# A decoder layer on one core: the token rows of the expert tiles, from the sixth tile on, turned by VectorE in squares of 32 instead of by TensorE

## The chip, the cores and the metric

The kernel runs on one core of one Trainium2 chip. A core has five engines that work through their own instruction streams and meet at semaphores: TensorE (PE, the matmuls), VectorE (DVE), ScalarE (ACT), GpSimd (POOL) and SyncE (SP), and 16 DMA engines that their queues feed. Data lies in SBUF (128 partitions) and the results of matmuls in PSUM (8 banks of 128 x 512 float32). The metric is the device time of the core in microseconds, smaller is better; the profile gives one execution of the program.

## The reference

A decoder layer on x of shape (8, 256, 256): self-attention with rotary embedding, cross-attention on a context of the same shape, and a feed-forward layer with 8 experts of which each token uses 2. Each of the three adds to x. The part that matters here is the third, on 2048 tokens of width 256:

```python
def _L0_ffn_ref(x, router_w, router_b, lang_w, lang_b, w1, b1, w2, b2):
    ...
    router_probs = jax.nn.softmax(router_logits, axis=-1)
    top_p, top_i = jax.lax.top_k(router_probs, TOP_K)
    top_p = top_p / top_p.sum(axis=-1, keepdims=True)
    h = jax.nn.gelu(jnp.einsum('bsd,edh->bseh', x, w1) + b1, approximate=False)
    expert_out = jnp.einsum('bseh,ehd->bsed', h, w2) + b2
    sel = jnp.take_along_axis(expert_out, top_i[..., None], axis=2)
    return (top_p[..., None] * sel).sum(axis=2)

x = x + _L0_ffn_ref(_layernorm(x, axis=-1), ...)
```

w1 is (8, 256, 1024), w2 (8, 1024, 256), all float32. The kernel computes the experts only for the tokens that chose them.

## The kernel before

Every engine walks the same table of numbered slots, made by `schedule()`, and for each slot emits its own part of the pieces that stand there. So the order of the pieces in the slots is the order of each engine's instructions; nothing is reordered later. Slots up to about 275 hold the attention of 16 units (8 batches, self and cross); the routing of the tokens and the expert tiles lie at the end.

The routing puts each token's row number on the list of its two experts. Tiles of 128 rows are cut from these lists: 39 tiles, each of one expert. Tiles 0 to 8 are cut after the first four batches, the others when all batches are routed. For tile n:

- `list` (SP): loads 128 row numbers and gates. `gather` (POOL, line 1484): an indirect DMA brings the 128 rows of width 256 into one of three buffers `x_rows`. Before it may overwrite a buffer, the turn of tile n - 3 must be over.
- `w1t` (ACT line 990 and DVE line 1270): each copies one half of the expert's w1 (128 x 1024) into one of two buffers `w1t`, reordered.
- `xturn` (PE line 857, ACT line 997): the rows have tokens on the partitions, the up-projection needs the 256 features there. TensorE turns the two halves of 128 x 128 by a product with the identity into a PSUM bank of a ring of three; ScalarE copies the bank to one of two buffers `xT`, once the up-projection of tile n - 2 is over.
- `up_a`, `up_b` (PE line 748): 32 float32 matmuls of 128 x 128, hidden = w1 x rows. They wait for `xT`, both halves of `w1t`, and the hidden bank. ACT line 1012 applies bias and gelu.
- `down_a`, `down_b` (PE line 755): 16 matmuls of 128 x 256 into a bank of the same ring.
- `moved_y` (DVE lines 1281 and 1287): adds the bias, multiplies by the gate. `add` (POOL line 1494): an indirect DMA adds the 128 rows to the output; each waits for the landing of the one before.

From slot 304 on the slots repeat, with j from 3 to 38 in slot 301 + j, in this order within a slot: list and gather of tile j + 4, w1t and xturn of tile j + 2, up of tile j + 1, down, moved_y and add of tile j. A text below says "up 5" for the up-projection of tile 5. Slot 304 also holds the last batch's `counted` (PE line 851), `table` (a chain of some 15 small VectorE instructions that ends at line 1219 and tells tiles 9 to 38 their expert and their place) and `listed` (POOL line 1424: eight indirect DMAs that write the lists), all ahead of the tile pieces.

`WARM` names places at which TensorE runs filler matmuls of the identity (line 634) whose results are overwritten; `fill()` emits them after it has the ring's bank. Among them are 4 ahead of down 6 and 10 ahead of the turn of tile 9. `Plan` numbers the uses of the ring; `filled` and `emptied` give the semaphore and the count for a use.

Of the kernel before, what the change touches and what calls it, by code (L numbers as in the profile page):

```python
# [15 lines left out]
P = 128  # L16
# [69 lines left out]
def rope_tables():  # L86
# [4 lines left out]
    for at in (position // 16, position % 16):  # L91
# [54 lines left out]
        "count", 1, 5), (8, "ot", 1, 6, 0), (2, "cturn", 1, 7), (4, "xturn", 2, 0), (5, "xturn", 2, 2), (4,  # L146
        "down_a", 2, 6), (10, "xturn", 2, 9), (8, "top", 3, 0), (3, "low", 13, 1))
AFTER_SELF = ((18, "xbias"),)
# [29 lines left out]

STEADY, STEADY_AT = 3, 304


# [98 lines left out]
class Plan:  # L280


    def __init__(self):
        self.slots = schedule()
        self.warm = {tuple(piece): many for many, *piece in WARM}
        rung = [p for s in self.slots for p in s.pieces if p[0] in RING]
        self.use = {p: i for i, p in enumerate(rung)}

        self.loaded, counts = {}, [0] * STACKS
        for unit in ORDER:  # L290
            i = POS[unit]
            counts[i % STACKS] += len(Q_LOADS) + len(K_LOADS) + (i >= MASKED)
            self.loaded[unit] = counts[i % STACKS]


class Memory:
# [128 lines left out]
    def signals(self):  # L425
# [32 lines left out]
        self.s_gather = [sem(f"tile_gather{i}") for i in range(X_RING)]  # L458
        self.s_list = [sem(f"tile_list{i}") for i in range(LIST_RING)]
        self.s_w1_v, self.s_w1_a = sem("tile_w1_vector"), sem("tile_w1_scalar")  # L460

# [154 lines left out]
def tensor_attention(m):  # L616
# [143 lines left out]
    for slot in plan.slots:  # L760
# [6 lines left out]
        for piece in slot.pieces:  # L767
# [79 lines left out]
            elif name == "counted":  # L847
# [4 lines left out]
                          stop=True).then_inc(m.fills(piece), 1)  # L852
            elif name == "xturn":
                bank = fill(piece)
# [5 lines left out]
            elif name == "up_a":  # L860
# [4 lines left out]
                if n == 1:  # L865
                    for w in range(B_RING):
                        pe.wait_ge(m.b_free[w], len(ORDER) * H // B_RING)
                pe.wait_ge(*m.emptied(("xturn", TILE, n)))
                pe.wait_ge(m.s_w1_v, n + 1)
# [29 lines left out]
def scalar_attention(m, out, rows, table):  # L899
# [45 lines left out]
    for slot in plan.slots:  # L945
        if slot.low is not None:
            exponentials(slot.low)
        for piece in slot.pieces:
# [29 lines left out]
            elif name == "w1t":  # L978
# [9 lines left out]
                else:  # L988
# [3 lines left out]
                         ).then_inc(m.s_w1_a, 1)  # L992
            elif name == "xturn":
                act.wait_ge(*m.filled(piece))
# [59 lines left out]
def vector_attention(m):  # L1054
# [176 lines left out]
    for slot in plan.slots:  # L1231
        if slot.top is not None:
            maxima(slot.top)
        for piece in slot.pieces:
# [26 lines left out]
            elif name == "w1t":  # L1261
# [6 lines left out]
                else:  # L1268
                    v.wait_ge(m.s_up, 2 * (n - 1))
                v.tensor_copy(m.w1t[n % 2][:, 1, :].rearrange("p (c q) -> p c q", c=FC),  # L1270
                              m.w1_sb[1][:, bass.ds(e, 1), :].rearrange("p a (q c) -> p (a c) q", c=FC)
                              ).then_inc(m.s_w1_v, 1)
            elif name == "moved_y":
                if n == 0:
# [77 lines left out]
def pool_attention(m, table, rows, out):  # L1352
# [112 lines left out]
    for slot in plan.slots:  # L1465
        for piece in slot.pieces:
# [8 lines left out]
            elif name == "gather":  # L1475
# [4 lines left out]
                if n == EARLY:  # L1480
                    pool.wait_ge(*m.stored(m.s_rows, B - 1))
                if n >= X_RING:
                    pool.wait_ge(*m.filled(("xturn", TILE, n - X_RING)))
# [84 lines left out]
```

## Time and profile before

| what | value |
|---|---|
| median of 3 runs | 726.67 us (723.82, 726.67, 730.84) |
| the profiled execution's own time | 728.32 us |
| its span, first to last instruction | 726.4 us |
| mean granted TensorE clock | 0.974 |
| busy: PE, ACT, DVE, POOL | 92%, 61%, 51%, 40% of the span |

Busy shares are means over the attention (to about 430 us, with some tile work from 402 us on) and the tiles (the rest). The granted clock is given as a share of 2.4 GHz; it has two levels, 1.00 and 0.50 (1.2 GHz).

### The profile page before, as it was taken

How to read it: one execution, taken by the hardware profiler on the slowest of the kernel's cores; microseconds unless marked ns; L12 is line 12 of the kernel's file. 1: busy time of each engine (PE TensorE's matmuls, PEld its weight loads, DVE VectorE, ACT ScalarE, POOL GpSimd, SP SyncE). 2: the span in 40 equal slices, each digit the busy share in tenths (PEclk: the TensorE clock that was granted, in tenths of full speed). 3: DMA queues.
4: the chain of work that ended last, by engine and by line, in shares of the span. 5: the costliest groups of instructions: out<-in, count | busy, mean ns of one | idle time of the engine just before them, and what ended most of it. 6: DMA issues, size and time to landing. Idle time of an engine off the chain costs nothing.

```text
span 726.4 us, 15766 instructions
## 1 busy us (share of the span) xinstructions
PE 670.2 (92%) x5090; PEld 526.9 (73%) x5090; DVE 367.1 (51%) x811; ACT 443.6 (61%) x880; POOL 291.4 (40%) x547
## 2 busy tenths in 40 slices
PE   7678899999999999979879799999999999999996
PEld 4445576666767666656546487888999999999995
DVE  2296787686877777758853334422222222222221
ACT  3444658576676777768536474865666666666661
POOL 4233325254332464624173363543434333333322
PEclk9799999999999999999989899999999999999999
DMA  5445355555455554774796552142212121212121
GB/s 132 145 118 161 112 132 160 143 163 154 137 138 159 167 162 149 196 206 135 221 236 79 174 148 52 23 37 41 42 33 44 31 45 31 44 30 45 30 30 23
DMA packets 55841, 78.26 MB, mean 108 GB/s; under 512 B 15374, under 2 KB 45297, under 8 KB 54737
## 3 DMA queue, kind: packets, MB, share of 16 engines
q1 hardware_dynamic: 42441, 62.37, 31.6%
q0 software_dynamic: 8512, 10.26, 9.2%
q10 hardware_dynamic: 4808, 4.61, 2.8%
q8 instruction: 43, 0.70, 0.4%
q14 instruction: 37, 0.30, 0.1%
HBM read 54.52 MB, written 22.35 MB: 106 GB/s over the span
## 4 chain that ended last, share of the span: by engine, by line
PE 70%; DVE 7%; POOL 5%; issue 5%; DMA 5%; ACT 4%; SPq 3%; ACTq 0%; DVEq 0%; POOLq 0%
PE attention_psum L748 18%; PE attention_psum L755 18%; PE attention_psum L740 7%; PE attention_psum L690 5%; PE attention_psum L709 5%; PE attention_psum L788 4%; PE attention_psum L645 3%; PE attention_psum L639 3%; DVE neg_max L1228 2%; PE attention_psum L634 2%; SPq L565 2%; DMA lists<-entry,place 2%; POOL lists L1424 1%; PE attention_psum L826 1%; PE attention_psum L857 1%
## 5 line engine op out<-in xcount | busy, mean ns | idle before, releaser
L916 ACT ACTIVATE weights<-attention_psum 128x512 f32<-128x512 f32 x256 | 147.7, 596 | 87.7 <-PE attention_psum L709 65.0
L1228 DVE TENSOR_REDUCE neg_max<-attention_psum 128x2 f32<-128x512 f32 x256 | 168.8, 685 | 54.2 <-PE attention_psum L690 53.7
L748 PE MATMUL attention_psum<-over,v 128*128 128x128 f32 x1248 | 146.4, 275 | 0.0
L748 PEld LDWEIGHTS attention_psum<-over,v 128*128 128x128 f32 x1248 | 143.1, 192 | 0.2
L755 PE MATMUL attention_psum<-weights 128*128 x624 | 143.2, 383 | 0.0
L1012 ACT ACTIVATE weights<-attention_psum,b_sb 128x128 f32<-128x128 f32 x312 | 89.0, 369 | 79.7 <-PE attention_psum L748 77.7
L1494 POOL DMA_INDIRECT out<-over x39 | 64.4, 1650 | 165.2 <-DVE over L1287 154.6
L755 PEld LDWEIGHTS attention_psum<-weights 128*128 128x128 f32 x624 | 117.0, 193 | 14.5
L690 PE MATMUL attention_psum<-weights 99*128 99x256 bf16 x512 | 99.9, 277 | 11.7 <-DVE neg_max L1228 10.9
L709 PE MATMUL attention_psum<-weights 102*128 102x256 bf16 (+1 forms) x512 | 104.0, 277 | 5.6 <-DMA weights<-maxT 4.9
L1281 DVE TENSOR_TENSOR over<-attention_psum,b_sb 128x256 f32<-128x256 f32 x39 | 16.6, 425 | 179.6 <-PE attention_psum L755 178.9
L990 ACT COPY v<-w_sb 128x1024 f32 x39 | 80.4, 2061 | 0.8 <-issue 0.6
L1503 POOL TENSOR_TENSOR weights<-weights 128x512 bf16<-128x512 f32 x32 | 36.9, 1157 | 107.4 <-ACT weights L1051 107.1
L690 PEld LDWEIGHTS attention_psum<-weights 99*128 99x128 bf16 x512 | 41.9, 99 | 51.6 <-DVE neg_max L1228 20.8
L740 PE MATMUL attention_psum<-weights,v 128*32 128x256 f32 x1024 | 76.3, 395 | 0.0
L709 PEld LDWEIGHTS attention_psum<-weights 102*128 102x128 bf16 (+1 forms) x512 | 50.3, 99 | 16.6 <-issue 5.8
L1270 DVE COPY v<-weights 128x1024 f32 x39 | 42.8, 1100 | 16.2 <-issue 14.5
L740 PEld LDWEIGHTS attention_psum<-weights,v 128*32 128x32 f32 x1024 | 31.1, 111 | 27.2 <-issue 14.9
L1484 POOL DMA_INDIRECT over<-rows,over x39 | 38.9, 998 | 23.1 <-DMA over<-lists 12.2
L634 PE MATMUL attention_psum<-identb 128*128 128x512 bf16 x168 | 43.1, 394 | 2.3 <-POOL identb L1367 2.3
L1424 POOL DMA_INDIRECT lists<-entry,place x32 | 32.9, 1027 | 15.2 <-issue 9.1
L639 PE MATMUL attention_psum<-ident,weights 128*128 128x128 f32 x160 | 25.6, 287 | 14.2 <-ACT weights L933 12.5
(168 smaller groups left out, 757.1 us busy)
## 6 DMA issues: line engine op xcount, KB each, us to landing
parts<-weights SPq DMA_DIRECT2D x96, 128.0 KB
weights<-parts SPq DMA_DIRECT2D x64, 192.0 KB
weights<-parts SPq DMA_DIRECT2D x64, 128.0 KB
weights<-in_L_ffn_w SPq DMA_DIRECT2D x8, 1024.0 KB, 9.2
weights<-parts SPq DMA_DIRECT2D x64, 64.0 KB
w_sb<-in_L_ffn_w SPq DMA_DIRECT2D x8, 512.0 KB
weights<-in_L_ffn_w SPq DMA_DIRECT2D x8, 512.0 KB
weights<-in_x SPq DMA_DIRECT2D x8, 256.0 KB, 3.2
```

The costliest lines, as they stand in the source:

```text
L634: pe.matmul(bank[:, :], m.identb[:, :], wide, start=True, stop=True)
L639: last = pe.transpose(bank[:, (c * T + t) * P:(c * T + t + 1) * P], rows[:, t, c * P:(c + 1) * P], m.ident[:, :])
L690: last = pe.matmul(bank[:, t * S:(t + 1) * S], q[0:MAX0, h % HALF, t * P:(t + 1) * P], k[0:MAX0, h % HALF, :], start=True, stop=True)
L709: last = pe.matmul(bank[:, t * S:(t + 1) * S], k[0:rows, h % HALF, t * P:(t + 1) * P], q[0:rows, h % HALF, :], start=True, stop=(i < SELEC ...
L740: last = pe.matmul(m.o_bank[32 * j:32 * j + 32, g * S:(g + 1) * S], v[:, t, head_at(h), :], m.p[:, u % P_RING, t * S:(t + 1) * S], start=( ...
L748: last = pe.matmul(m.hT_bank[j % 2][:, c * P:(c + 1) * P], m.w1t[j % 2][:, k, c * P:(c + 1) * P], m.xT[j % 2][:, k, :], start=(k == 0), st ...
L755: last = pe.matmul(m.bank_of(("down_a", TILE, j))[:, 0:D], m.hidT[j % HIDDEN][:, c, :], m.w2_sb[:, bass.ds(expert, 1), c, :].rearrange("p ...
L916: act.activation(m.p[:, u % P_RING, :], m.b_bank[u % B_RING], ACT.Exp, scale=SCALE[ORDER[u // H][0]]).then_inc(m.b_free[u % B_RING], 1)
L990: act.copy(m.w1t[n % 2][:, 0, :].rearrange("p (c q) -> p c q", c=FC), m.w1_sb[0][:, bass.ds(e, 1), :].rearrange("p a (q c) -> p (a c) q", ...
L1012: last = act.activation(m.hidT[n % HIDDEN][:, c, :], m.hT_bank[n % 2][:, c * P:(c + 1) * P], ACT.Gelu, bias=m.b1_sb[:, bass.ds(gelu_expert ...
L1228: v.tensor_reduce(m.neg_max[:, :, h:h + 1], m.a_bank[u % A_RING].rearrange("p (t k) -> p t k", t=T), AXX, ALU.max, negate=True).then_inc(m ...
L1494: pool.indirect_dma_start(out=known(out, n), out_offset=tokens(n), in_=m.y_gated[n % 2], in_offset=None, compute_op=ALU.add).then_inc(m.s_ ...
```

## The change

For tiles 5 to 38 the piece `xturn` is no longer TensorE's and ScalarE's. VectorE turns the gathered rows straight from `x_rows` to `xT` with 16 transposes: each takes the rows of 32 tokens and, in both halves of the features, 32 columns (32 partitions x 2 x 32) and writes them turned. It waits for the gather and for the up-projection of tile n - 2 once, ahead of the sixteen; the last one counts up a new semaphore. TensorE's up-projection waits for that semaphore instead of the ring's, and so does POOL's gather that reuses the buffer. These tiles' turns leave the ring of three banks, and the ten fillers ahead of tile 9's turn are deleted. Tiles 0 to 4 stay as they were.

```diff
-        "down_a", 2, 6), (10, "xturn", 2, 9), (8, "top", 3, 0), (3, "low", 13, 1))
+        "down_a", 2, 6), (8, "top", 3, 0), (3, "low", 13, 1))
...
+SQUARES = 5
+QUAD = 32
...
-        rung = [p for s in self.slots for p in s.pieces if p[0] in RING]
+        rung = [p for s in self.slots for p in s.pieces
+                if p[0] in RING and not (p[0] == "xturn" and p[2] >= SQUARES)]
...
+        self.s_squares = sem("tile_rows_turned")
... (TensorE)
-            elif name == "xturn":
+            elif name == "xturn" and n < SQUARES:
...
-                pe.wait_ge(*m.emptied(("xturn", TILE, n)))
+                if n < SQUARES:
+                    pe.wait_ge(*m.emptied(("xturn", TILE, n)))
+                else:
+                    pe.wait_ge(m.s_squares, n - SQUARES + 1)
                 pe.wait_ge(m.s_w1_v, n + 1)
... (ScalarE)
-            elif name == "xturn":
+            elif name == "xturn" and n < SQUARES:
... (VectorE)
+            elif name == "xturn" and n >= SQUARES:
+
+                v.wait_ge(m.s_gather[n % X_RING], 16 * (n // X_RING + 1))
+                v.wait_ge(m.s_up, 2 * (n - 1))
+                x = m.x_rows[n % X_RING][:, :].rearrange("p (c q) -> p c q", c=KC)
+                for r in range(0, P, QUAD):
+                    for q in range(0, P, QUAD):
+                        last = v.transpose(m.xT[n % 2][q:q + QUAD, :, r:r + QUAD], x[r:r + QUAD, :, q:q + QUAD])
+                last.then_inc(m.s_squares, 1)
... (POOL)
-                if n >= X_RING:
+                if n >= SQUARES + X_RING:
+                    pool.wait_ge(m.s_squares, n - X_RING - SQUARES + 1)
+                elif n >= X_RING:
                     pool.wait_ge(*m.filled(("xturn", TILE, n - X_RING)))
```

TensorE's order at slot 304, after down 2 and the count of the last batch. `ident` and `over` are the identity and the area that holds `x_rows` and `xT`; `v` holds `w1t`. Before:

```order
L851 MATMUL attention_psum<-before,ones 128x8 [waits counts_before,ring_free1]
L857 MATMUL attention_psum<-ident,over 128x128 [waits tile_gather2,ring_free2]
L857 MATMUL attention_psum<-ident,over 128x128
L748 MATMUL attention_psum<-over,v 128x128 [waits tile_w1_scalar,tile_gelu,tile_w1_vector,ring_free1]
L748 MATMUL attention_psum<-over,v 128x128 x15
L882 TENSOR_LOAD over [waits ring_free0]
```

And with the change, whose line numbers are 5 to 8 higher:

```order
L856 MATMUL attention_psum<-before,ones 128x8 [waits counts_before,ring_free1]
L753 MATMUL attention_psum<-over,v 128x128 [waits tile_w1_scalar,tile_gelu,tile_w1_vector,ring_free1]
L753 MATMUL attention_psum<-over,v 128x128 x15
L890 TENSOR_LOAD over [waits ring_free2]
L890 ISA x2
```

The turn of tile 5 (line 857) has gone from between the count and up 4. Up 5 and all later ones carry the wait `tile_rows_turned` in place of the ring's.

VectorE's order at the same slot, from the end of the routing table to the result of tile 3. `weights` holds w1's second half. Before:

```order
L1219 TENSOR_TENSOR over<-start,over 128x30 [waits dve_chain]
L1265 TENSOR_LOAD over [waits routed]
L1265 ISA x2
L1270 ISA [waits tile_up]
L1270 COPY v<-weights 128x1024
L1276 TENSOR_LOAD over
L1276 ISA x2
L1281 ISA [waits tile_gated,ring_full0]
L1281 TENSOR_TENSOR over<-attention_psum,b2_sb 128x256
L1287 TENSOR_SCALAR over<-over 128x256 [waits tile_add,ring_free0]
```

With the change:

```order
L1227 TENSOR_TENSOR over<-start,over 128x30 [waits dve_chain]
L1273 TENSOR_LOAD over [waits routed]
L1273 ISA x2
L1278 ISA [waits tile_up]
L1278 COPY v<-weights 128x1024
L1288 STREAM_TRANSPOSE over<-over 32x2x32 [waits tile_up,tile_gather2]
L1288 STREAM_TRANSPOSE over<-over 32x2x32 x15
L1293 TENSOR_LOAD over
L1293 ISA x2
L1298 ISA [waits tile_gated,ring_full2]
L1298 TENSOR_TENSOR over<-attention_psum,b2_sb 128x256
L1304 TENSOR_SCALAR over<-over 128x256 [waits tile_add,ring_free2]
```

The sixteen transposes stand between the weight copy of a tile and the result of the tile two before it, here and in each later slot; in slot 304 they also stand behind the whole routing table.

## Rows read from the trace of the kernel before

**Rows 1.** The page, busy time, share of the span and instructions
```profile
PE 670.2 (92%) x5090; PEld 526.9 (73%) x5090; DVE 367.1 (51%) x811; ACT 443.6 (61%) x880; POOL 291.4 (40%) x547
```

**Rows 2.** Chain that ended last, 430 to 726: start, length in us, what
```profile
446.16 5.24 PE attention_psum L755 x16
...
460.65 3.58 PE attention_psum L748 x32
...
467.91 3.57 PE attention_psum L748 x32
...
485.98 0.86 PE attention_psum L634 x4
...
490.29 2.16 PE attention_psum L634 x10
492.67 3.57 PE attention_psum L748 x32
...
499.92 3.57 PE attention_psum L748 x32
...
702.85 3.57 PE attention_psum L748 x32
...
709.88 3.57 PE attention_psum L748 x32
```

**Rows 3.** Timeline of one tile: start, us, engine, line, what, [idle before]
```profile
601.31 0.42 DVE L1281 TENSOR_TENSOR over<-attention_psum,b_sb 128x256 f32<-128x256 f32 x1 [4.94 <-PE attention_psum L755]
...
602.52 1.10 DVE L1270 COPY v<-weights 128x1024 f32 x1 [0.40 <-issue]
...
608.56 0.42 DVE L1281 TENSOR_TENSOR over<-attention_psum,b_sb 128x256 f32<-128x256 f32 x1 [4.93 <-PE attention_psum L755]
```

**Rows 4.** Timeline around slot 304
```profile
457.47 2.02 ACT L990 COPY v<-w_sb 128x1024 f32 x1
...
460.21 0.44 PE L857 MATMUL attention_psum<-ident,over 128*128 128x128 f32 x2 [1.35 <-DVE over L1281]
...
464.07 0.21 DVE L1219 TENSOR_TENSOR over<-start,over 128x30 int32<-128x30 f32 x1
465.06 1.09 DVE L1270 COPY v<-weights 128x1024 f32 x1 [0.78 <-DVE over L1219]
```

**Rows 5.** VectorE's groups by form: ... | busy us, mean ns | idle before
```profile
L1297 DVE TENSOR_TENSOR over<-weights,over 128x128 f32<-128x128 f32 x32 | 7.8, 286 | 0.0
...
L1062 DVE TENSOR_TENSOR over<-upto,over 128x64 f32<-128x64 f32 x2 | 0.5, 227 | 0.1
```

**Rows 6.** Timeline of VectorE, two operations that do not wait for one another
```profile
33.09 0.49 DVE L1297 TENSOR_TENSOR over<-weights,over 128x128 f32<-128x128 f32 x2
```

**Rows 7.** Timeline, the gather of tile 9
```profile
488.20 1.02 POOL L1484 DMA_INDIRECT over<-rows,over  x1 [0.30 <-issue]
```

**Rows 8.** Line 1484, all gathers, from issue to landing
```profile
DMA to landing us min/median/max: 2.7/2.9/5.6
```

**Rows 9.** Timeline of TensorE around idle times
```profile
362.18 0.39 PE L690 MATMUL attention_psum<-weights 99*128 99x256 bf16 x2
...
365.90 0.61 PE L690 MATMUL attention_psum<-weights 99*128 99x256 bf16 x2 [3.11 <-DVE neg_max L1228]
...
407.20 1.12 PE L857 MATMUL attention_psum<-ident,over 128*128 128x128 f32 x4 [3.56 <-DMA over<-rows,over]
408.11 0.42 PE L709 MATMUL attention_psum<-weights 99*128 99x256 bf16 x1
...
413.89 0.27 PE L709 MATMUL attention_psum<-weights 99*128 99x256 bf16 x1
...
445.13 1.03 PE L645 MATMUL attention_psum<-r_sb,rowsT 128*128 128x12 f32 x8 [1.43 <-ACT rowsT L943]
```

**Rows 10.** Windows: stretch, length, busy PE PEld DVE ACT POOL, PEclk, DMA
```profile
447.00:450.00 3.00, 3.00 (x8) 2.37 (x7) 2.07 (x12) 0.54 (x2) 0.00 (x0) 0.50 0.00 0
```

**Rows 11.** Chain that ended last, near its end
```profile
718.32 3.64 DMA out<-over
```

## The prediction

> **What bounds the kernel now.** I read the page first: TensorE is busy for 670.2 us, 92% of the span [rows 1]. That is a mean over two programs, so I went on to the chain of the work that ended last. From 460 us on it is TensorE alone: 32 matmuls of line 748 (the up-projection of a tile), 16 of line 755 (the down-projection of the tile before), again and again [rows 2]. The reader should look at the starts. Up-projection of tile 9 starts at 499.92, of tile 37 at 702.85: 28 intervals of 7.248 us. Up-projection of tile 38, ahead of which no rows are turned, starts at 709.88, so 7.03 us later. The difference, 0.218 us, is what two turns of line 857 cost on the path. The timeline of one tile then shows how much room VectorE has: it sat idle for 4.93 us before line 1281 [rows 3].
>
> **What is removed.** Tiles 5 to 38 are turned by VectorE, 34 tiles. From up 9 to up 38 there are 28 turns (tiles 11 to 38): 28 x 0.218 = 6.10 us. Between up 5 (467.91) and up 9 (499.92) lie 32.01 us, four tiles with four turns, 4 fillers of line 634 (0.86 us) and 10 more (2.16 us) [rows 2]. The ten are the ones that the change deletes. What stays is 4 x 7.03 + 0.86 = 28.98, a gain of 3.03 us. The ten were cover for the wait on the gather of tile 9. That gather is issued at 488.20 and lands 2.9 us later at the median, 5.6 at most, so by 491.1 or at worst 493.8 [rows 7, 8]. In the new order VectorE waits for it while TensorE goes on with up 8 and down 7, so no filler is needed: nothing is put back for it. ScalarE loses the copies of line 997; it waits for TensorE in any case, and I cost them at nothing.
>
> **What is added: x, the time of 16 transposes.** The trace has no VectorE transpose. Each moves 32 partitions x 64 elements. The nearest rows are the 128x64 operations at 227 ns each, one waiting for the other, and the 128x128 operations of line 1297 at 286 ns [rows 5]. Two of line 1297 that do not wait for one another take 0.49 us and not 0.57 [rows 6]: the second starts 0.20 us after the first, 0.08 less than its length. The 59 ns between 227 and 286 are the 64 extra columns, so without a wait a 64-column operation should come every 0.20 - 0.06 = 0.14 us. The sixteen write apart and wait only once. Low end: 15 x 0.14 + 0.23 = 2.3 us. If nothing overlaps: 16 x 0.227 = 3.6 us. If besides each column takes two turns: 16 x 0.286 = 4.6 us. I take x = 2.6 us, 0.16 each, near the low end, because the pair that the trace has without a wait does overlap; the rest is for filling and emptying a square. Here a page speaks against the change. The Trainium skill (VectorE: DVE Perf Modes, section "The TRN2 errata") has a fixed cost per instruction on SBUF sources that many small tiles pay each time, measured at about 150 cycles beside one cycle a column. By it x is an estimate of 16 x 214 cycles at 0.96 GHz = 3.6 us. The sum would be 10.7 - 3.6 = 7.1 us by it. The trace agrees for operations that wait for one another (227 ns) and not for the pair of line 1297.
>
> **Does VectorE keep up?** From the start of line 1281 to the end of line 1270 it is 603.62 - 601.31 = 2.31 us [rows 3]. The register load ahead of the next line 1281 is about 0.4 us, as the one ahead of line 1270. So a tile costs VectorE 2.7 + x against 7.03 on TensorE. With x = 2.6 that is 5.3: hidden. The limit is x = 4.3, or 0.27 us a transpose. The gather of tile n + 4 on POOL now waits for VectorE's turn of tile n + 1, a whole tile earlier, and the queue behind it (the adds of line 1494, on which line 1287's buffer depends) keeps its time.
>
> **The one place where it is not hidden** is the first turned tile, 5. Its transposes stand in VectorE's order behind the routing table (line 1219) and the weight copy of line 1270, which ends at 465.06 + 1.09 = 466.15 [rows 4]. TensorE before did this turn at 460.21, after the wait for line 1281. Without it up 4 waits only for ScalarE's weight copy, 457.47 + 2.02 = 459.49, so it starts some 0.9 us sooner. Its 3.57 us and 3.46 us of down 3 (7.03 less 3.57) end at 466.6. Up 5 cannot start before the transposes end: 466.15 + x, plus 0.2 for the semaphore and for the chain's start of a row, is 466.35 + x, against 467.91. That costs x - 1.56 and leaves TensorE idle for about x - 0.3, 2.3 us. VectorE then has tile 6 ready 0.8 + 0.4 + 1.1 + x after up 5 starts, which is 4.9 of 7.03: late only once.
>
> **The sum.** 6.10 + 3.03 + 1.56 - x = 10.7 - 2.6 = 8.1 us. Behind the last matmul nothing changes: the last add waits for the DMA of the one before it (718.32 + 3.64 = 722.0) [rows 11], and both follow TensorE's end as now. Against the profiled execution: 728.32 - 8.1 = 720.2 us. That execution stands 1.65 above the median of the three runs, 726.67, and the runs themselves spread from 723.82 to 730.84, so I take the mean of the four times, 727.4, and forecast 719.3 us.
>
> **Rivals.**
>
> *The new idle time lowers the clock.* After an idle time of 3.56 us the trace shows the low level, matmuls of line 709 at 0.42 us rather than 0.27, and after 3.11 us too, the pair of line 690 in 0.61 us rather than 0.39 [rows 9]; after only 1.43 us, with eight small matmuls behind it, it does too: the granted clock of 447 to 450 is 0.50 (1.2 GHz and not 2.4) and the sixteen matmuls of line 755 take 5.24 us instead of 3.46 [rows 2, 9, 10]. Against it: behind the 1.35 us idle ahead of 460.21 up 4 took 3.58 us, as every other [rows 2, 4]. 2.3 us lies between. Price: 1.78 us for one such stretch, so 721.1; two cost 3.6 us.
>
> *Nothing overlaps.* Then x = 3.6: the sum is 7.1 and the time 720.3. But TensorE is idle for 3.3 us, about what brought the low clock both times above, so with one stretch 5.3 and 722.1. VectorE still has 0.7 us to spare in a tile. For it: all chained rows; against it: the pair of line 1297. This is the page's rule of above, as this kernel would feel it.
>
> *VectorE becomes the bound.* One mechanism, one point: x over 4.3 us. Each of the 33 tiles behind the first then takes 2.7 + x. At x = 4.6 the sum is 10.7 - 4.6 - 33 x 0.27 = -2.8: 730.2. At x = 5.0 it is -16.4: 743.8. It is slower than before by 1% from x = 4.7, 0.295 us each. For it: no row prices a square of 4-byte elements that has to be filled before it is emptied. Against it: that would be twice the spacing of any row of that size here.
>
> *The turn is not what ended the wait.* Up 5 to up 9 rest on lists and gathers that POOL and SP deliver late (the eight scatters of line 1424 and two adds stand ahead of gather 9). If a gather comes so late that VectorE, and so up 9 or up 10, waits, the 2.16 us of the fillers come back as idle time and with it a stretch of low clock: 10.7 - 2.6 - 2.2 - 1.8 = 4.1, 723.3. Against it: up 9 is due at 466.35 + x + 28.98 = 497.9, while the latest landing 493.8 + x is 496.4.
>
> **How the numbers follow.** My case 0.40, the lower clock 0.22, no overlap 0.20, VectorE as the bound 0.10, the late gather 0.08. The range takes all but most of VectorE as the bound: below, x = 2.3 on the lowest run, 723.8 - 8.4 = 715.4, above, x = 4.3 with two stretches of low clock, 727.4 - 6.4 + 3.6 = 724.6; I give 714.5 to 725. One per cent, about what a measurement of this kernel can tell from no change, is 7.3 us. My case is over it by 0.8 only, which the spread of the runs and x can undo: faster by over 1%: 0.44, within 1%: 0.47, slower: 0.09.
>
> **What would show it.** In the changed profile: starts of line 748's successor 7.03 us apart from up 6 on; VectorE busy with a group of 544 transposes; their spacing near 0.16 us; one idle time of about 2.3 us on TensorE near 467 us, released by VectorE; no filler at 490. I am wrong if the spacing of the tiles exceeds 7.1 us, if that idle time is over 3.5 us, if the clock is low behind it, or if a second idle time stands ahead of up 9.

## The result, and the profile after

| | before | with the change |
|---|---|---|
| median, 13 runs each | 729.06 us | 724.22 us |
| lowest to highest | 723.82 to 731.18 | 720.74 to 727.57 |
| span of the profiled execution | 726.4 us | 721.6 us |
| mean granted TensorE clock | 0.974 | 0.976 |
| busy: PE, ACT, DVE, POOL | 92%, 61%, 51%, 40% | 92%, 60%, 68%, 40% |

The ratio of the two kernels' runs is 0.9941, 95% interval 0.9923 to 0.9959: faster by 0.6%, so within the 1% that I had set as the bound. The sum of the prediction was 8.1 us; the two profiled executions differ by 4.8. The page of the changed kernel (busy us and share; then line, engine, operation, count, busy us, mean ns, idle time before):

```profile
PE 660.9 (92%) x5012; PEld 521.1 (72%) x5012; DVE 492.3 (68%) x1355; ACT 431.6 (60%) x846; POOL 291.9 (40%) x547
...
L753 PE MATMUL attention_psum<-over,v 128*128 128x128 f32 x1248 | 148.1, 277 | 4.0 <-DVE over L1288 3.1
...
L1288 DVE STREAM_TRANSPOSE over<-over 32x64 f32<-32x64 f32 x544 | 128.2, 236 | 7.0
```

VectorE has the 544 transposes, 236 ns each. TensorE waited for them (the last column of the second line) 3.1 us in all, and that was one single wait. The chain that ended last shows where (line 753 is an up-projection, 760 a down-projection, 639 fillers); it answers to [rows 2]:

```profile
446.28 5.24 PE attention_psum L760 x16
...
470.24 5.46 PE attention_psum L753 x32
475.71 3.46 PE attention_psum L760 x16
479.16 3.57 PE attention_psum L753 x32
...
486.19 3.57 PE attention_psum L753 x32
489.76 0.86 PE attention_psum L639 x4
...
494.08 3.57 PE attention_psum L753 x32
...
501.10 3.57 PE attention_psum L753 x32
...
704.88 3.57 PE attention_psum L753 x32
...
713.32 3.67 DMA out<-over
```

The tiles are 7.03 us apart, the ten fillers are gone, and nothing waits ahead of up 9. Up 5 is the exception: 5.46 us where every other one in these rows takes 3.57. The timeline around it (start, length, what, [idle before]) shows both of its troubles; its last line is from a late tile, where VectorE has 0.83 us to spare:

```profile
458.81 0.17 PE L856 MATMUL attention_psum<-before,ones 128*128 128x8 bf16 x1
...
459.87 3.81 PE L753 MATMUL attention_psum<-over,v 128*128 128x128 f32 x32 [0.89 <-ACT v L998]
...
465.20 1.10 DVE L1278 COPY v<-weights 128x1024 f32 x1 [0.78 <-issue]
...
466.21 3.98 DVE L1288 STREAM_TRANSPOSE over<-over 32x64 f32<-32x64 f32 x16
...
470.24 5.46 PE L753 MATMUL attention_psum<-over,v 128*128 128x128 f32 x32 [3.11 <-DVE over L1288]
...
606.65 0.42 DVE L1298 TENSOR_TENSOR over<-attention_psum,b_sb 128x256 f32<-128x256 f32 x1 [0.83 <-PE attention_psum L760]
```

The sixteen took 3.98 us, not 2.6, so TensorE stood idle for 3.11 us; and behind that its clock was low. The windows of four microseconds (length, busy us of PE, PEld, DVE, ACT, POOL, then the granted clock, DMA share, GB/s):

```profile
466.00:470.00 4.00, 1.14 (x6) 0.66 (x4) 3.79 (x17) 2.04 (x2) 3.09 (x4) 1.00 0.01 1
470.00:474.00 4.00, 3.76 (x22) 3.76 (x23) 3.45 (x11) 0.14 (x1) 3.33 (x3) 0.66 0.05 5
474.00:478.00 4.00, 4.00 (x24) 3.72 (x24) 2.32 (x10) 2.17 (x9) 2.60 (x2) 0.91 0.57 22
```

So x was 1.4 us longer than taken, and the clock cost 5.46 - 3.57 = 1.89 us. The prediction's sum with these two is 10.7 - 4.0 - 1.9 = 4.8 us, the difference of the spans.

**A common mark.** Executions differ by several us in the attention part, which the change does not touch: the `counted` matmul of the last batch (the first row of the timeline above) starts at 458.69 in the profile of before and at 455.81 to 461.53 in those of the experiments; the lowest of these belongs to a kernel whose attention part is that of before. So I compare the stretch from that matmul to the end of the span:

| kernel | counted | end | between | what differs |
|---|---|---|---|---|
| before | 458.69 | 726.4 | 267.7 | |
| the change | 458.81 | 721.6 | 262.8 | VectorE turns from tile 5 on |
| before_no_fill | 455.81 | 723.0 | 267.2 | before, without the ten fillers |
| cover | 459.70 | 721.0 | 261.3 | the change, 14 fillers ahead of up 5 |
| first_by_pe | 458.12 | 718.9 | 260.8 | VectorE from tile 6 on |
| first_by_pe_late | 460.79 | 721.7 | 260.9 | the same, tile 5 turned later |
| from_eight | 459.00 | 718.0 | 259.0 | VectorE from tile 8 on |
| wide | 459.97 | 717.9 | 257.9 | the change, 4 transposes a tile |
| copies | 459.42 | 721.5 | 262.1 | the change, copies for transposes |
| same_quadrant | 461.53 | 721.6 | 260.0 | the change, within the quadrants |
| crossing_fixed | 459.71 | 719.6 | 259.9 | the change, one quadrant further |
| q_outer | 459.38 | 721.8 | 262.4 | the change, loops swapped |
| diagonal | 456.82 | 719.5 | 262.6 | the change, by distance |
| halves | 460.89 | 736.1 | 275.2 | the change, 32 transposes a tile |

### The profile page after: what moved, and what is told of

Its sections match the earlier page's. It is cut to its first block, busy times and chain, and to the rows that moved or that the text cites. A ratio compares the mean times of both kernels' runs of the same rounds, so it can differ in the third digit from the quotient of the medians.

```text
span 721.6 us, 16087 instructions
## 1 busy us (share of the span) xinstructions
PE 660.9 (92%) x5012; PEld 521.1 (72%) x5012; DVE 492.3 (68%) x1355; ACT 431.6 (60%) x846; POOL 291.9 (40%) x547
## 4 chain that ended last, share of the span: by engine, by line
PE 71%; DVE 8%; issue 6%; POOL 5%; ACT 4%; DMA 2%; another core or an unknown queue 1%; SPq 1%; ACTq 1%; DVEq 0%; POOLq 0%
PE attention_psum L753 18%; PE attention_psum L760 17%; PE attention_psum L745 8%; PE attention_psum L695 6%; PE attention_psum L714 5%; PE attention_psum L793 4%; PE attention_psum L650 3%; PE attention_psum L644 3%; PE attention_psum L639 3%; DVE neg_max L1236 2%; PE attention_psum L831 2%; POOL rstd L1414 1%; PE attention_psum L803 1%; POOL tmp L1414 1%
## 5 line engine op out<-in xcount | busy, mean ns | idle before, releaser
L753 PEld LDWEIGHTS attention_psum<-over,v 128*128 128x128 f32 x1248 | 147.2, 194 | 6.5 <-DVE over L1288 3.5
L753 PE MATMUL attention_psum<-over,v 128*128 128x128 f32 x1248 | 148.1, 277 | 4.0 <-DVE over L1288 3.1
L1288 DVE STREAM_TRANSPOSE over<-over 32x64 f32<-32x64 f32 x544 | 128.2, 236 | 7.0
L639 PE MATMUL attention_psum<-identb 128*128 128x512 bf16 x158 | 41.0, 397 | 2.3 <-POOL identb L1384 2.3
```

Source lines behind the costliest of these rows:

```text
L639: pe.matmul(bank[:, :], m.identb[:, :], wide, start=True, stop=True)
L753: last = pe.matmul(m.hT_bank[j % 2][:, c * P:(c + 1) * P], m.w1t[j % 2][:, k, c * P:(c + 1) * P], m.xT[j % 2][:, k, :], start=(k == 0), st ...
L1288: last = v.transpose(m.xT[n % 2][q:q + QUAD, :, r:r + QUAD], x[r:r + QUAD, :, q:q + QUAD])
```

## Why sixteen transposes take 3.98 us

A quadrant is a group of 32 partitions that starts at 0, 32, 64 or 96. Two theories stood at the start: the transposes overlap little because a transpose is a different operation from the elementwise ones of [rows 5, 6]; or because of how these ones change their quadrants from one to the next.

**Copies in their place.** The same sixteen in shape and place, without the turning.

```diff
-                        last = v.transpose(m.xT[n % 2][q:q + QUAD, :, r:r + QUAD], x[r:r + QUAD, :, q:q + QUAD])
+                        last = v.tensor_copy(m.xT[n % 2][q:q + QUAD, :, r:r + QUAD], x[r:r + QUAD, :, q:q + QUAD])
```

> The sixteen transposes of a tile become sixteen copies of the same shape, places and types: the squares are moved but not turned, so the experts see wrong rows. It asks why the transposes came 0.249 us apart and not 0.16. Theory (a transpose does not overlap with its neighbour, a copy does): copies come 0.14 us apart, sixteen in 2.3 us; the idle time ahead of up 5 falls from 3.1 to about 1.9 us and up 5 starts at 468.6. Rival (operations of 32 partitions that read one quadrant and write another do not overlap, whatever they do): 0.24 to 0.25 us apart, as the transposes.

Measured: 723.71 us once, beside 728.16 of the kernel before. Up 5 and a tile's sixteen in the timeline:

```profile
470.30 5.47 PE L753 MATMUL attention_psum<-over,v 128*128 128x128 f32 x32 [2.56 <-DVE over L1288]
...
601.90 3.37 DVE L1288 COPY over<-over 32x64 f32<-32x64 f32 x16
```

That is 0.21 us each, where I had expected 0.14: turning adds 0.04 us to a copy that does not overlap either. Up 5 waited 2.6 us and ran at the low clock, in 5.47 us. The missing overlap is no matter of transposes.

**The same transposes within their quadrants.**

```diff
-                        last = v.transpose(m.xT[n % 2][q:q + QUAD, :, r:r + QUAD], x[r:r + QUAD, :, q:q + QUAD])
+                        last = v.transpose(m.xT[n % 2][r:r + QUAD, :, q:q + QUAD], x[r:r + QUAD, :, q:q + QUAD])
```

> Each transpose writes the 32 partitions that it reads (squares are turned in place of their quadrant and not moved, so the experts see wrong rows). Theory (the price is the transpose's own): 0.249 us apart as before, sixteen in 4.0 us. Rival (the move between quadrants costs): under 0.2 us apart.

Measured: 723.77 us once, beside 728.16. The timeline, at a late tile and at up 5:

```profile
601.71 2.50 DVE L1288 STREAM_TRANSPOSE over<-over 32x64 f32<-32x64 f32 x16
...
471.48 3.84 PE L753 MATMUL attention_psum<-over,v 128*128 128x128 f32 x32 [1.62 <-DVE over L1288]
```

The sixteen take 2.50 us, close to the 2.6 of the prediction, for instructions of the same kind, size and number; the theory that I had put first (4.0 us again) is wrong, its rival right. So the places decide. Here four in a row read one quadrant and write one; in the change the written quadrant is another at each. But this edit alters two things, that the neighbours keep their quadrants and that nothing crosses from one quadrant to another.

**Four instructions over all 128 partitions.**

```diff
-                for r in range(0, P, QUAD):
-                    for q in range(0, P, QUAD):
-                        last = v.transpose(m.xT[n % 2][q:q + QUAD, :, r:r + QUAD], x[r:r + QUAD, :, q:q + QUAD])
+                for q in range(0, P, QUAD):
+                    last = v.transpose(m.xT[n % 2][:, :, q:q + QUAD], x[:, :, q:q + QUAD])
```

> Four transposes over all 128 partitions in a tile instead of sixteen over 32 (the squares stay in their quadrant, so the experts see wrong rows). Theory (a transpose's price does not depend on the partitions): 0.249 us each, 1.0 us a tile; up 5 starts at about 467.3, TensorE idle for 0.7 us and at full clock, gain against the kernel before 9.5 to 10 us. Rival: each takes four times as long and nothing is won over the change.

Measured: 720.25 us once, beside 728.16; the four took this long:

```profile
605.03 0.61 DVE L1287 STREAM_TRANSPOSE over<-over 128x64 f32<-128x64 f32 x4
```

0.15 us each, as in the run before over 32 partitions (0.16): the number of partitions costs nothing. I had expected 0.25 us each, the spacing of the change. Up 5 did not wait (461.02 for up 4, 468.29 for up 5) and took 3.57 us. From the count to the end it is 257.9 us: the change's 262.8 less 4.9, about the 3.11 us of idle time and the 1.89 us of clock. So 4.9 us is what a cure of the wait alone can give.

**Two instructions for each, one for each half of the features.**

```diff
-                        last = v.transpose(m.xT[n % 2][q:q + QUAD, :, r:r + QUAD], x[r:r + QUAD, :, q:q + QUAD])
+                        for c in range(KC):
+                            last = v.transpose(m.xT[n % 2][q:q + QUAD, c, r:r + QUAD], x[r:r + QUAD, c, q:q + QUAD])
```

> Each transpose is split into its two squares: 32 of 32x32 in a tile instead of 16 of 32x64. It gives the fixed part of the price and drives VectorE over its limit. Theory: fixed part 0.17 to 0.18 us and 1.04 ns a column, so 0.21 to 0.22 us each, 6.8 to 7.0 us a tile; VectorE then needs 2.7 + 6.9 = 9.6 us a tile against 7.03 on TensorE, the tiles come 9.4 to 9.8 us apart, and the time is some 75 to 95 us over the kernel before. Rival one (the price goes with the columns): 0.125 us each, no tile is slower than in the change. Rival two: VectorE over its limit still hides part, spacing under 8.5 us.

Measured: 738.50 us once, beside 728.16: 1.4% slower. The timeline, read from four starting points, each one instruction later than the last:

```profile
603.99 4.94 DVE L1289 STREAM_TRANSPOSE over<-over 32x32 f32<-32x32 f32 x32
604.12 4.82 DVE L1289 STREAM_TRANSPOSE over<-over 32x32 f32<-32x32 f32 x31
604.29 4.64 DVE L1289 STREAM_TRANSPOSE over<-over 32x32 f32<-32x32 f32 x30
604.42 4.51 DVE L1289 STREAM_TRANSPOSE over<-over 32x32 f32<-32x32 f32 x29
```

The starts are 0.13 us apart within a pair of one place and 0.17 from pair to pair. Both my theory (0.21 us each and 75 to 95 us over the kernel before) and its rival (0.125 us each, no tile slower) missed: it is 0.15 us each and 10 us over. At x = 4.94 VectorE is the bound. Up 5 in the chain, behind 4.06 us of idle time, and two up-projections near its end, two tiles apart:

```profile
473.27 6.77 PE attention_psum L753 x32
...
689.89 3.84 PE attention_psum L753 x32
...
704.56 3.84 PE attention_psum L753 x32
```

The two are 14.67 us apart, so 7.33 us a tile: 4.94 and 2.4 for the rest. In the timeline the tiles take turns: in one VectorE waits for nothing and needs 2.25 us beside the transposes, in the next it waits 0.3 us for a down-projection. The rival of the prediction is real, but by an estimate from these two it begins between x = 4.65 (7.03 - 2.4) and 4.8 (7.03 - 2.25), not at 4.3: I had added a register load of 0.4 us that runs beside the transposes.

**Two other orders of the change's own sixteen.** First the loops swapped, so that four in a row write one quadrant and read four:

```diff
-                for r in range(0, P, QUAD):
-                    for q in range(0, P, QUAD):
+                for q in range(0, P, QUAD):
+                    for r in range(0, P, QUAD):
```

> The same sixteen transposes as in the change in another order: the 32 columns are the outer loop, so that four in a row write the same quadrant of 32 partitions and read four different ones. Theory A (a transpose waits out the one before it where the two write to different quadrants): twelve of the fifteen neighbours then come 0.151 us apart as in the run within one quadrant, three 0.249, and the sixteen take about 12 x 0.151 + 3 x 0.249 + 0.24 = 2.8 us instead of 3.98; up 5 then waits less than 2 us for VectorE and runs at full clock, some 3 us of span less than the change. Theory B (what counts is that the quadrant read changes, or that source and destination differ at all): 4.0 us again and up 5 at 5.46 us after 3.1 us of idle time.

Then by the distance from the read to the written quadrant:

```diff
-                for r in range(0, P, QUAD):
-                    for q in range(0, P, QUAD):
+                for d in range(0, P, QUAD):
+                    for r in range(0, P, QUAD):
+                        q = (r + d) % P
```

> The same sixteen transposes, ordered by the distance from the quadrant read to the quadrant written: first the four that stay in their quadrant, then the four that move by one, by two, by three. Theory A (neighbours that write to different quadrants don't overlap): 4.0 us a tile, as with the change. Theory C (what must be waited out is a change of the distance, the routing between the quadrants, which stays the same for four in a row here): about 2.8 us. Theory D (a transpose overlaps the one before only where it stays in its own quadrant): the first four come 0.151 us apart, the other twelve 0.249, together 3 x 0.151 + 12 x 0.249 + 0.24 = 3.7 us.

Measured: 724.08 and 721.80 us, once each, beside 731.95. The timelines of VectorE, of the one and of the other:

```profile
602.17 3.97 DVE L1288 STREAM_TRANSPOSE over<-over 32x64 f32<-32x64 f32 x16
```

```profile
606.77 3.97 DVE L1289 STREAM_TRANSPOSE over<-over 32x64 f32<-32x64 f32 x16
607.00 3.73 DVE L1289 STREAM_TRANSPOSE over<-over 32x64 f32<-32x64 f32 x15
...
```

3.97 us in both, and up 5 waited 3.1 us and took 5.21 and 5.35 us. The single times are 2.3 us apart, but from the count to the end it is 262.4 and 262.6 us. It is not enough that the written quadrant stays; it is not enough that the distance stays; and even the first four of the second order, which stay in their quadrant as those in the run above, do not overlap, 0.23 us from the first to the second, because the neighbour is in another. All three theories of mine for a better order (A, C and D) fell. What was left is that both quadrants have to stay, or that something in crossing forbids the overlap.

**Crossing, with both quadrants kept for four in a row.**

```diff
-                    for q in range(0, P, QUAD):
-                        last = v.transpose(m.xT[n % 2][q:q + QUAD, :, r:r + QUAD], x[r:r + QUAD, :, q:q + QUAD])
+                    to = (r + QUAD) % P
+                    for q in range(0, P, QUAD):
+                        last = v.transpose(m.xT[n % 2][to:to + QUAD, :, q:q + QUAD], x[r:r + QUAD, :, q:q + QUAD])
```

> The sixteen transposes of each tile each write one quadrant further than they read (rows 0 to 31 to partitions 32 to 63 and so on), four in a row with the same two quadrants. The rows' blocks land in other places than the experts need, so the tile's result isn't the reference's; number and size of the instructions are the change's. Theory E (a transpose starts early behind the one before only where both read the same quadrant and both write the same one; crossing as such costs little): within four in a row about 0.13 us apart as in the run within one quadrant, and about 0.25 where the quadrants change: 12 x 0.13 + 3 x 0.25 + 0.24 = 2.5 us for sixteen, up 5 waits about 1.6 us for VectorE and runs in 3.8 us. Theory F (crossing as such forbids the overlap): 3.98 us, up 5 at 5.46 us.

Measured: 721.90 us once, beside a median of 726.57. The timeline, from successive instructions on, and up 5:

```profile
599.87 2.51 DVE L1289 STREAM_TRANSPOSE over<-over 32x64 f32<-32x64 f32 x16
600.04 2.34 DVE L1289 STREAM_TRANSPOSE over<-over 32x64 f32<-32x64 f32 x15
...
600.29 2.09 DVE L1289 STREAM_TRANSPOSE over<-over 32x64 f32<-32x64 f32 x13
600.50 1.88 DVE L1289 STREAM_TRANSPOSE over<-over 32x64 f32<-32x64 f32 x12
...
469.78 3.84 PE L753 MATMUL attention_psum<-over,v 128*128 128x128 f32 x32 [1.74 <-DVE over L1289]
```

Sixteen in 2.51 us, all of them crossing. The second, third and fourth start 0.17, 0.12 and 0.13 us after the one before; the fifth, the first of the next pair of quadrants, 0.21 us after. That settles it: a transpose starts while the one before it still runs only where it reads the same quadrant as that one and writes the same one. Crossing as such is free. The Trainium skill says just this (VectorE: DVE Perf Modes, section "Two Vector instructions with no wait between them"): an instruction is held until all earlier ones of VectorE have finished when its input starts in another quadrant than the last read did, or its output in another than the last write. The runs agree in every order tried. I had not weighed that rule in the prediction; by it "nothing overlaps" was the likeliest case from the start, since the change alters the written quadrant fifteen times.

This run is also the prediction's own case, with x = 2.51: TensorE idle for 1.74 us, full clock behind it, and 267.7 - 259.9 = 7.8 us gained from the count to the end, beside 10.7 - 2.5 = 8.2 by the prediction's sum. The rest of the sum stands, then. (The single time, 4.7 us under the median of before, can't tell: the eleven runs of before beside it spread over 6.7 us.)

A turn of 128 x 128 needs all sixteen pairs of read and written quadrant, each once, so no order of sixteen can keep both. 3.98 us is the price of this form.

## Was it the wait at up 5, and its clock?

**Fillers in the gap.** 14 filler matmuls ahead of up 5, in the bank that up 5 then fills.

```diff
+COVER = 14
...
+                if n == SQUARES:
+                    pe.wait_ge(m.s_gelu, 2 * (n - 1))
+                    for _ in range(COVER):
+                        pe.matmul(m.hT_bank[n % 2][:, 0:BANK], m.identb[:, :], wide, start=True, stop=True)
```

> The change, with 14 filler matmuls in the idle time ahead of up 5. Theory: the idle time of 3.1 us brought the low clock, so with the fillers up 5 takes 3.57 us instead of 5.46 and still starts at 470.2: 1.9 us better than the change, gain 6.7 us against the kernel before. Rival (the slow up 5 comes from VectorE's or the queue's traffic and not from the idle time): up 5 stays at 5.4 us or so, no gain over the change.

Measured: 720.60 us (6 runs), 17 of before at 728.59; ratio 0.9879, interval 0.9847 to 0.9910. The chain:

```profile
471.11 3.84 PE attention_psum L754 x32
...
478.40 3.57 PE attention_psum L754 x32
```

Up 5 starts 11.41 us after the count, with the change it was 11.43; but it takes 3.84 us and not 5.46. From the count to the end 1.5 us are gained. So the idle time is what lowered the clock, and the clock alone is worth 1.5 to 1.6 us (5.46 - 3.84). The ratio is better than the change's by 0.6%, or 4.5 us, more than that. The two were measured at different times, and the profiled execution of this kernel (723.34 us) lies 2.7 us over its median, that of the change (723.94) 0.3 under its own. The stretch from the count shows no more than the 1.5; what the rest is I can't say.

**The ten fillers taken out of the kernel before.**

```diff
-        "down_a", 2, 6), (10, "xturn", 2, 9), (8, "top", 3, 0), (3, "low", 13, 1))
+        "down_a", 2, 6), (8, "top", 3, 0), (3, "low", 13, 1))
```

> The kernel before without the ten fillers ahead of the turn of tile 9. It asks what their deletion is worth by itself. Theory: the gather of tile 9 lands at about 491.1, the turn starts there instead of 492.3, so about 1.0 to 1.2 us of the 2.16 are won, unless the idle time lowers the clock, which would cost up to 1.9. Rival one: the rows are there already at 490.1, all 2.16 us are won. Rival two: nothing is won, the fillers just filled the wait to its end.

Measured: 726.38 us (10 runs); ratio 0.9976, interval 0.9953 to 1.0000. In their place stands a wait for the gather (the chain, then the turn of tile 9 in the timeline):

```profile
485.48 2.87 DMA over<-rows,over
488.89 3.71 PE attention_psum L748 x32
...
496.27 3.57 PE attention_psum L748 x32
```

```profile
488.48 0.41 PE L857 MATMUL attention_psum<-ident,over 128*128 128x128 f32 x2 [1.05 <-DMA over<-rows,over]
```

From the count to up 9 it is 40.46 us and was 41.23: of the 2.16 us of fillers 0.8 was gained. 1.05 turned into that wait, and 0.3 went because the turn and up 8 no longer follow another matmul without a pause. The clock stayed full without them. So the fillers stood in a real wait, but ran on beyond it: 0.8 us of their 2.16 could be had in the kernel before, and 1.4 are a gain only together with the change, which lets VectorE do the waiting: with it TensorE has no wait there.

## Versions that leave the first tiles to TensorE

**Tile 5 turned as before.**

```diff
-SQUARES = 5
+SQUARES = 6
```

> Tile 5 is left to TensorE, tiles 6 to 38 are turned by VectorE. Theory (the loss is one late turn: sixteen transposes of 0.25 us behind the routing table, 3.1 us of idle TensorE and 1.9 us of low clock behind it): up 5 starts at about 467.7 us instead of 470.2, at full clock, no idle time of TensorE over 1 us near 467. From there 7.03 us a tile. Gain against the kernel before: 3.03 + 6.10 + 0.2 = 9.3 us, a ratio of about 0.987, and 4.6 us better than the change. Rival (the missing gain is spread over all tiles, since a busier VectorE slows something in each): the spacing of the tiles is the same here and the gain stays under 6 us.

Measured: 718.12 us (6 runs), 17 of before at 728.59; ratio 0.9846, interval 0.9819 to 0.9873. Up 5 is no longer late: up 4 starts at 460.09, up 5 at 467.22, up 8 at 491.35. But another wait appeared, at up 7. The timeline:

```profile
473.99 1.15 ACT L1020 ACTIVATE weights<-attention_psum,b_sb 128x128 f32<-128x128 f32 x4 [3.65 <-remote]
474.08 4.03 PE L753 MATMUL attention_psum<-over,v 128*128 128x128 f32 x32
...
476.94 0.42 DVE L1298 TENSOR_TENSOR over<-attention_psum,b_sb 128x256 f32<-128x256 f32 x1 [3.28 <-remote]
...
479.17 3.97 DVE L1288 STREAM_TRANSPOSE over<-over 32x64 f32<-32x64 f32 x16
...
483.19 3.84 PE L753 MATMUL attention_psum<-over,v 128*128 128x128 f32 x32 [1.62 <-DVE over L1288]
```

ScalarE waited for the second half of up 5, whose matmuls were over by 470.8, until 473.99; VectorE waited for down 4, over by 474.3, until 476.94. "remote" is the profile's word for an end of a wait that it cannot put down to an engine. With VectorE this late, its 3.97 us of transposes became TensorE's wait. From up 5 to up 8 it is 24.13 us instead of 3 x 7.03 + 0.86 = 21.95. The expectation had the late turn right (up 5 on time and at full clock, 2.0 us less than the change from the count to the end, of 4.6 expected), and did not have this wait.

**The same with tile 5's turn a place later in the order**, behind up 4, where its wait for line 1298 should cost nothing.

```diff
+            if j == STEADY and name == "down_a":
+                slots[STEADY_AT].pieces.append(("xturn", TILE, STEADY + 2))
+            if (j, name) == (STEADY, "xturn"):
+                continue
```

> As the run before it, and TensorE turns tile 5 behind up 4 instead of ahead of it. Theory: ahead of up 4 the turn waited for a bank that VectorE empties late (line 1281), 0.6 to 0.9 us; behind up 4 it waits for nothing. Up 4 starts at 459.9, up 5 at about 467.1: another 0.6 us, gain 9.9 us against the kernel before, ratio 0.986. Rival: ScalarE's copy of the turned rows now stands behind the gelu of tile 4 and is late, up 5 starts at 467.7 or later, no gain over the run before it.

Measured: 722.46 us (6 runs), ratio 0.9895, interval 0.9859 to 0.9931. Up 4 starts 1.07 us after the count instead of 1.83, as meant; but from the count to the end it is 260.9 us, as without the edit, because the wait ahead of up 7 was 1.8 us and the same two late wake-ups (3.9 and 3.5 us) stand in this profile. No gain to be seen. The median is 4.3 us higher than that of the version without the edit, for the same stretch: so far apart can six runs of two kernels lie without a cause in this part, and a difference of medians of this size says little here.

**VectorE from tile 8 on.**

```diff
-SQUARES = 5
+SQUARES = 8
```

> The change, but TensorE and ScalarE turn the rows of tiles 5, 6 and 7 too, and VectorE those from tile 8 on. Against the version in which VectorE starts with tile 6 it has two more turns on TensorE, 2 x 0.22 = 0.4 us. Theory A (the 1.6 us that up 7 waited there came from VectorE's 4 us of transposes behind a late start): tile 7's rows are turned by ScalarE in 0.4 us, the wait shrinks to under 0.5 us, and the time from up 5 to up 8 falls from 24.1 to about 22.7 us; 0.8 us less span from the count to the end than its 260.8. Theory B (ScalarE and VectorE are both held up by the late signal, and TensorE would wait for gelu or the ring anyway): from up 5 to up 8 24 us or more, 261.2 us or more from the count to the end. In both it is faster than the kernel before by 0.8 to 1.3%.

Measured: 716.77 us (6 runs), 11 of before at 726.57; ratio 0.9855, interval 0.9824 to 0.9886. The waits of TensorE from 436 us on, all of them (waiting line, what ended it, us in total, times, longest), and the chain:

```profile
PE attention_psum L650 <- ACT rowsT L951: 1.4, 1, 1.4
PE attention_psum L862 <- DVE over L1298: 1.4, 1, 1.4
```

```profile
468.22 3.57 PE attention_psum L753 x32
...
475.47 3.57 PE attention_psum L753 x32
...
482.49 3.57 PE attention_psum L753 x32
...
490.38 3.57 PE attention_psum L753 x32
```

No transpose is waited for any more; from up 5 to up 8 it is 22.16 us. This profile has no late wake-up, so the comparison does not tell whether the earlier turns would have hidden one. From the count to the end it is 259.0 us, 3.8 less than the change and 1.8 less than the version from tile 6 on. The two intervals overlap: I call both better than the change (1.5% faster than before, where the change is 0.6% faster) and do not rank them.

## Why the prediction missed

- **Up-projections 7.03 us apart from up 6 on** held: 28 of the intervals, 6.1 us.
- **The ten fillers and four turns ahead of up 9**, 3.03 us, held, and no wait took their place. The run without the fillers in the kernel before showed a wait of 1.05 us there: 1.4 of their 2.16 us are the change's own, 0.8 could be had without it.
- **Up 4 sooner by 0.9 us**: up 4 starts 1.06 us after the count and started 1.80 after it before (460.49 - 458.69 in the timeline), so 0.74 sooner. Behind its wait it took 3.81 us and not 3.57.
- **x, the time of sixteen transposes: this step failed.** Forecast 2.6, measured 3.98, 15 x 0.249 + 0.24. The prediction read the overlap off the pair of line 1297 [rows 6] and said that "the sixteen write apart". That is exactly what forbids it: the pair reads and writes in the same partitions, the sixteen change the quadrant each time. Its upper bound "nothing overlaps", 16 x 0.227 = 3.6, was the right mechanism, with a chance of 0.20 only, and still 0.35 us short, since one transpose takes 236 ns and the next starts 13 ns after its end. With the quadrants kept, x was 2.51 and the gain 7.8 us from the count to the end.
- **Full clock as the likeliest: this failed with it.** Idle for x - 0.3 = 2.3 us was forecast; x = 3.98 made it 3.11, and up 5 took 1.89 us more (forecast price 1.78). Some 0.27 of it is not the clock, since an up-projection behind any wait of TensorE at full clock shows 3.84 us and not 3.57; the low level is worth 5.46 - 3.84 = 1.6. The formula x - 0.3 itself was off: it gives 3.7 at x = 3.98, and 2.2 at the 2.5 of two runs whose idle times were 1.62 and 1.74. Up 4 and down 3 ended later than forecast, and of the 0.2 us for the semaphore only 0.05 was there. The rival "Nothing overlaps" had both failures together at 5.3 us of gain and 722.1 us; measured 4.8.
- **VectorE keeps up**: it did, with 0.83 us to spare ahead of line 1298 where 4.93 had been [rows 3]. Its need beside the transposes is 2.2 to 2.4 us, not 2.7, and the limit 4.65 to 4.8, not 4.3.
- **The gather of tile 9**: no wait, as forecast. **The end**: 3.67 us of the last DMA wait and 3.64 before [rows 11], as forecast; from up 38 to the end it is 16.7 us and was 16.5.

Of 8.1 us the two failed terms took 1.4 + 1.9 = 3.3. That the corrected sum meets the 4.8 to a tenth is in part luck: up 5 came 0.2 us sooner than x - 1.56 says, and the end took 0.2 more. The forecast of 719.3 us stood on a level of 727.4 for the kernel before; over more runs it was 729.06, which is the rest of the way to 724.22.

## What to carry to other kernels

Price short VectorE instructions in a row by where they start: 32 x 64 float32 transposes come some 0.13 us apart while the quadrant read and the quadrant written stay the same (0.16 to 0.17 from the first to the second). Where either changes, the next one waits for the end of the one before: 0.25 us apart where it changes each time, 0.21 at a change after four alike; a pair elsewhere in the trace is a fair measure only if it keeps or changes its partitions in the same way. Where work moves to another engine, the steady state may hide it wholly and its first instance not at all: leave the first tiles, which stand behind a long chain on that engine, where they were. And price a new idle time on TensorE together with the clock behind it.

## What the runs showed of the hardware that I had not expected

- **Clock behind an idle time.** Behind 1.62, 1.74 and 1.82 us an up-projection took 3.84 us, at full clock (1.82 is up 7 of first_by_pe_late). Behind 2.56 us (copies) it took 5.47, behind 3.1 us 5.46, 5.21 and 5.35 (the change, q_outer, diagonal), with a granted clock of 0.66 in the change's four microseconds from 470 on, and behind 4.06 us (halves) 6.77, with 0.58 and 0.57 in the two stretches of four from 472 on. With 14 fillers in a gap of the same place, 3.84. The length of the idle time alone does not decide. All fourteen profiles have the idle time of 1.41 to 1.45 us with eight small matmuls behind it, in the attention part [rows 9]; in eight of them, the kernel before among them [rows 10], the sixteen matmuls that follow took 4.93 to 5.24 us, in the other six 3.55. So what the prediction took from that place as a case of the low clock falls out differently from one execution to another.
- **Partitions cost nothing.** Where they overlap, four transposes of 128 x 64 take 0.61 us, 0.15 each, and sixteen of 32 x 64 take 2.50, 0.16 each.
- **Late wake-ups.** In seven of the twelve kernels of the experiments (both from tile 6 on, cover, copies, same_quadrant, q_outer, diagonal) ScalarE, and in three of them VectorE too, went on only 1.8 to 5.1 us after the matmuls that it waited for were over, between 473 and 481 us, where it is 0.14 us in the kernel with four transposes; the profile names no releaser. The eight list scatters of POOL end at about that time, but they do in the profiles without the effect too. It cost TensorE 1.6 and 1.8 us of waiting ahead of up 7 in the two versions from tile 6 on, and 0.3 and 0.6 us inside up 6 (4.03 and 4.36 us in the timeline, for 3.73); in the other five at most 0.25 us is to be seen (up 6 of same_quadrant, 3.98 us). Its cause is open; no run here isolates it.
